# Linear attention stage: another order of the same steps, and constant products at other places

## The reference

```python
mix_in = tanh((x + xx * maa_x) @ maa_w1)            # xx = previous row - row
xrg, xwa, xk, xv = x + xx * (maa + mix)             # four mixed inputs
r, k, v, g, kk, a, ... = products of these          # "features"
def step(S, inp):                                   # per head, 64x64 state
    sa = einsum('bhij,bhj->bhi', S, at)
    S = S * exp(w) + sa * bt + vt * kt
    return S, einsum('bhij,bhj->bhi', S, rt)
y = layernorm_per_head(scan(step)) * ln_w + ln_b + (sum(r*k*faaaa)) * v
out = (y * g) @ w_output.T
```

## Time and profile before

| | |
|---|---|
| median of 3 runs | 3612.98 us (3612.59 to 3615.72) |
| time of the profiled execution | 3623.5 us |
| its span, first to last instruction | 3621.8 us |
| PE, DVE, ACT, POOL busy | 83%, 70%, 50%, 29% of the span |
| mean granted PE clock | 0.912 |
| `stage_c`, first product to last step | 1762 to 3184 us of the span |
| I0 of unit 0 to I9 of unit 15 | 1828 to 3126 us |

### The profile page before, as it was taken

The page is one execution under the profiler, slowest core; times in us unless marked ns, Lnnn a source line. Parts: engine busy times, 40 slices in busy tenths (PEclk is TensorE's granted clock), DMA queues, the critical chain, the costliest instruction groups (busy, mean ns, idle before and its releaser), DMA issues.

```text
span 3621.8 us, 117698 instructions
## 1 busy us (share of the span) xinstructions
PE 3013.2 (83%) x51890; PEld 1965.8 (54%) x51890; DVE 2536.8 (70%) x5294; ACT 1820.5 (50%) x3063; POOL 1047.3 (29%) x1164
## 2 busy tenths in 40 slices
PE   6889999998648898988578888888888887779995
PEld 4555555555325555554245555555555555458774
DVE  3666666665549888888467777787777776457774
ACT  3334444444438878887244444454454552246661
POOL 0332122122531111222232332233333332045552
PEclk8899899899769999999789998899999997789997
DMA  2227999200043444330200000000000000056666
GB/s 75 79 97 304 395 394 319 30 1 1 33 138 128 137 143 140 129 126 21 70 3 4 12 11 9 10 10 13 10 10 10 10 12 14 9 190 228 224 214 180
DMA packets 161678, 356.92 MB, mean 99 GB/s; under 512 B 13821, under 2 KB 98559, under 8 KB 154896
## 3 DMA queue, kind: packets, MB, share of 16 engines
q1 hardware_dynamic: 147088, 323.95, 26.3%
q0 software_dynamic: 14080, 25.45, 2.1%
HBM read 136.33 MB, written 216.67 MB: 97 GB/s over the span
## 4 chain that ended last, share of the span: by engine, by line
PE 54%; DVE 21%; ACT 12%; issue 9%; DMA 2%; SPq 1%; another core or an unknown queue 1%; POOL 1%; DVEq 0%; POOLq 0%; ACTq 0%
PE ps L1551 7%; PE ps L135 4%; PE ps L137 4%; PE ps L136 4%; DVE t L485 3%; PE ps L1616 3%; PE ps L342 2%; PE ps L896 2%; ACT t L1035 2%; ACT t L1033 2%; PE ps L346 2%; PE ps L903 2%; PE ps L298 1%; PE ps L304 1%; DVE t L522 1%
## 5 line engine op out<-in xcount | busy, mean ns | idle before, releaser
L1551 PE MATMUL ps<-t 128*128 128x512 f32 x608 | 345.5, 682 | 49.7 <-DVE t L2056 13.0
L241 POOL TENSOR_SCALAR_AFFINE_SELECT t<-t 128x512 f32<-128x512 f32 x256 | 168.6, 659 | 663.4 <-ACT t L425 663.4
L485 DVE TENSOR_REDUCE t<-ps 128x2 f32<-128x512 f32 (+1 forms) x512 | 260.7, 551 | 116.5 <-PE ps L304 116.3
L135 PE MATMUL ps<-t 128*128 128x512 f32 (+1 forms) x660 | 280.6, 425 | 60.1 <-DVE t L511 34.9
L425 ACT ACTIVATE t<-ps 128x768 f32<-128x768 f32 x256 | 206.8, 808 | 213.1 <-PE ps L330 213.1
L137 PE MATMUL ps<-t 128*128 128x512 f32 (+1 forms) x660 | 258.5, 392 | 0.0
L136 PE MATMUL ps<-t 128*128 128x512 f32 (+1 forms) x660 | 258.2, 391 | 0.0
L1361 POOL DMA_INDIRECT deltas<-t x92 | 94.4, 1026 | 507.1 <-DVE t L1307 484.9
L2794 POOL DMA_INDIRECT answers<-t x156 | 153.9, 987 | 160.3 <-DVE t L2765 122.4
L1551 PEld LDWEIGHTS ps<-t 128*128 128x128 f32 x608 | 111.5, 207 | 142.9 <-issue 75.5
L135 PEld LDWEIGHTS ps<-t 128*128 128x128 f32 x660 | 128.4, 194 | 110.5 <-DVE t L511 42.9
(11 more groups left out here) (443 smaller groups left out, 8359.8 us busy)
## 6 DMA issues: line engine op xcount, KB each, us to landing
paired<-t SPq DMA_DIRECT2D x14, 8384.0 KB, 59.9
t<-experts SPq DMA_DIRECT2D x39, 1536.0 KB
sorted<-t SPq DMA_DIRECT2D x22, 1950.0 KB, 8.8
t<-in_wP SPq DMA_DIRECT2D x92, 320.5 KB, 3.5
experts<-t SPq DMA_DIRECT2D x8, 1536.0 KB, 6.0
t<-sorted SPq DMA_DIRECT2D x39, 260.0 KB
t<-answers SPq DMA_DIRECT2D x16, 512.0 KB, 6.7
t<-in_wE SPq DMA_DIRECT2D x8, 768.0 KB, 7.6
```

The lines of the kernel that those rows point to most:

```text
L135: pe.e.matmul(out, a[0], b[0], start=start, stop=False, skip_group_check=True)
L241: pool.e.affine_select(own, own, [[0, 2], [0, 2], [1, 128]], ALU.is_ge, 0.0, base=0, channel_multiplier=-1).then_inc(*kept(b, j))
L485: m = dve.e.tensor_reduce(nmf[:, z, blk * 16 + 4 * g + i0:blk * 16 + 4 * g + i0 + 2], ps[:, k:k + 2, a0:a1], AX.X, ALU.max, negate=True)
L1551: pe.e.matmul(ps[out, k, :], lhs, rhs, start=True, stop=True).then_inc(*e_pe(u, name))
```

## The change

The two tables get other numbers, nothing else. Every step, its instructions and its waits stay; the places, and so the order on each engine, are others. The first place of a unit is -228 and the last 316, so it lives for 544 places and not for 589. The constant products go from 7 with 1,536 columns for a unit to 11 with 2,944: I2 from (0, 0, 128, 0) to (384, 384, 256, 128), I9 from (384, 0, 0, 0) to (128, 0, 256, 0), the state scan from (384, 128, 128, 256, 128, 0) to (256, 0, 384, 384, 256, 0), and 128 columns at the selection's ranks.

```diff
-AT = {"E": (-243, -236, -219, -216, -208, -198, -188, -183, -179, -170, -162, -151, -147, -138, -136, -133, -132,
-           -131, -122, -121, -120, -116, -114, -113, -111, -108, -102, -99, -91),
-      "L": ((-97, -94, -93, -89, -84, -75, -72, -69, -66, -65, -63, -58, -56, -55, -48, -47, -46),
-            (-40, -37, -35, -34, -30, -29, -28, -25, -23, -22, -16, -15, -14, -8, -2, -1, 14)),
-      "I": ((-26, -20, -19, -11, -6, 1, 9, 13, 20, 29),
-            (3, 10, 12, 21, 28, 35, 42, 52, 58, 71),
-            (38, 50, 51, 59, 65, 76, 81, 87, 95, 105),
-            (79, 85, 86, 96, 102, 111, 117, 120, 126, 134)),
-      "S": (142, 153, 157, 161, 164, 172, 175, 181, 184, 191, 194, 200, 202, 205, 212, 215, 222, 227, 232, 237, 238,
-           245, 259, 266, 269, 271, 273, 284, 287, 307, 308, 324, 331, 337, 346)}
-HOLD = {"tp": (0, 0, 128, 0), "bd": (384, 0, 0, 0), "s": (384, 128, 128, 256, 128, 0),
-        "fc": 0, "rl": 0, "rk": 0}
+AT = {"E": (-228, -220, -210, -206, -200, -197, -193, -186, -174, -165, -160, -154, -146, -137, -130, -128, -123,
+           -122, -121, -119, -114, -108, -101, -100, -97, -94, -92, -91, -87),
+      "L": ((-85, -84, -81, -80, -74, -70, -57, -56, -51, -50, -49, -45, -43, -41, -40, -35, -33),
+            (-32, -31, -30, -28, -25, -24, -23, -20, -18, -11, -7, -4, -3, -2, 0, 6, 28)),
+      "I": ((-21, -14, -13, -10, -1, 5, 13, 27, 34, 42),
+            (12, 25, 26, 31, 35, 45, 52, 62, 69, 77),
+            (50, 60, 61, 67, 72, 78, 86, 94, 101, 109),
+            (84, 91, 92, 99, 104, 112, 119, 126, 132, 140)),
+      "S": (149, 152, 158, 167, 177, 181, 187, 193, 197, 201, 203, 209, 211, 212, 213, 218, 223, 234, 238, 259, 261,
+           267, 271, 279, 280, 283, 285, 294, 297, 298, 299, 308, 309, 312, 316)}
+HOLD = {"tp": (384, 384, 256, 128), "bd": (128, 0, 256, 0), "s": (256, 0, 384, 384, 256, 0),
+        "fc": 0, "rl": 0, "rk": 128}
```

## The result

On the chip of the first measurement the kernel after takes 3682.53 us (median of 4, 3675.58 to 3704.9) and the kernel before 3614.35 us (median of 4): a ratio of 1.0196, 95% interval 1.0157 to 1.0234. It is 2% slower. The forecast was 3585 us, with a range that ended at 3628.

A forecast was written before the change was run, and what follows sets the result against it. PE's order was taken to bound the kernel. Terms a unit: +2.6 - 1.9 - 1.2 - 1.5 = -2.0 us; over 14 units -28 us off the 3612.98 us median, so 3585 us, range 3558 to 3628.

The forecast's parts named there:

- The failed step: Linear attention stage: steps, transfers and waits only move, POOL's scatters with them; no term in the sum.
- nearly all these gaps: PE's "issue" gaps, 96 us in the steady stretch, nearly all at the same place in a row of 256 instructions.
- What bounds the kernel: Linear attention stage: PE's order sets the 82.4 us a unit; DVE has 20 us to spare.
- Constant products: 1,408 more columns a unit on PE: +2.6 us if paid in full, bounds 0 and 5.2.
- rival A: Constant products paid in full, little given back: +2.0 us a unit, 3641 us; above 3620 us, chance 0.23.
- Fetch gaps: Moved constant products fill PE's waits for instruction fetches: -1.9 us a unit, bounds 0 and -2.6.
- The scaling by 7.9 / 13.5: Cuts the fetch-gap gain from -2.2 to -1.3 us a unit, since waits and slow clock fill part.
- Clock: Fewer thin stretches of PE work, 4 of 9.9 us leave the lower clock: -1.2 us a unit, bounds 0 and -4.9.
- Waits: PE's waits for other engines: 3.9 us a unit go, half kept, 0.5 charged: -1.5, bounds +1.0 and -3.9.
- the list of tight pairs: Places where PE has less work between a result and its use, among them DVE's copies and the tanh (0.3 us).
- Ends: First and last units' serial chains at the stage's ends: 0 change, within 5 us either way.
- Rival C: Clock nearly always full, waits nearly gone: -6.0 us a unit, 3529 us; below 3560 us, chance 0.12.

The follow-up runs named there:

- the bunched runs: Kernel before with its last seven S places side by side at 287 to 293: 3675.59 us (1.0117) on chip 3, 3666.48 us (1.0134) on chip 12.

## Why the prediction failed, point by point

**The failed step** is "No step, instruction of a step or transfer is added or removed; POOL's scatters and all waits are moved with their steps", which gave the moved scatters no term in the sum. POOL stands there with 316 busy us of 1000 and no more. What a scatter does to PE wasn't asked, though seven of the eight had moved into one row beside small products. On the first chip that is +9.4 us a unit at I0 of tile 1, more than all terms of the forecast together; behind it the clock has fallen to 0.50. Undone alone, on chip 3, it gives back 1.0025 in place of 1.0196 on the first chip (no run of the unchanged kernel after stands in that group, so the step between the two, 1.7%, is across chips). Done alone it costs 1.17 and 1.34%. None of the rivals had this mechanism. The trace of before did show it, faintly: 26 of its 98 longer "issue" gaps, 12 us in 1000, are not at the place of the fetches, and all 26 lie beside a scatter. The prediction's "nearly all these gaps" (87% of their time) passed over them. The number of matmuls alone gives no warning: 12.1 in a scatter's 1.26 us (18.1 on chip 4), mostly beside products over all 128 rows, which take their time anyway.

The other steps can be read where the scatters cost nothing, on chip 4 (per unit; idle and busy of the windows times the period over 1000):

| | forecast | chip 4 | first chip |
|---|---|---|---|
| "issue" waits of PE | -1.9 | 6.9 to 3.2: **-3.7** | 7.9 to 9.8: **+1.9** |
| waits for other engines | -1.5 | 3.8 to 2.7: **-1.2** | 4.3 to 0.9: **-3.4** |
| constant products and clock, PE busy | +2.6 - 1.2 | 69.7 to 70.1: **+0.4** | 69.9 to 76.8: **+6.9** |
| sum = change of the period | -2.0 | **-4.6** | **+5.3** |

- *What bounds the kernel*: right. Of the 76.2 us of a unit after on chip 4, PE is busy for 70.1 and DVE, the next fullest, for 61.9.
- *Constant products*, "+2.6 us a unit if paid in full": with the table after and its scatters at 339 to 385 they cost nothing on chip 6 (0.9876 with the new, 0.9877 with the old). Their columns fall into time in which PE would have waited for instructions (its issue waits are 53.9 us with the new and 68.0 with the old in 1000) or run in the lower clock. On the table before, on chip 3, they cost 0.9 us a unit, and beside the slow I0 perhaps more (1.0196 against 1.0130, across chips): there rival A may be true in part.
- *Fetch gaps*: the direction was right and the size too small, even against the unscaled -2.2. The scaling by 7.9 / 13.5 for waits that fill part of the short runs made it smaller still. The gaps at every 256th instruction fell on the first chip as well, by the table above from 82 x 0.0824 = 6.8 to 33 x 0.0877 = 2.9 us a unit; the +1.9 there is this and 12 x 0.0824 = 1.0 to 75 x 0.0877 = 6.6 us beside scatters.
- *Clock*: 0.95 to 0.96 on chip 4. Time in the lower clock falls from (1 - 0.95) x 2 x 80.8 = 8.1 to 6.1 us a unit; work of 2.0 us there takes 1.0 above. -1.0 against -1.2: right, within the two digits of the view (the clock records of the two traces give 8.8 to 5.7 us, so -1.6). On the first chip it goes the other way, 9.9 to 19.3 us, as the stall at I0 comes every unit and full products and state products behind it run at half speed.
- *Waits*: those named all went. On the first chip more than forecast went, as one would expect of a PE that loses 9 us at one place and is late everywhere else. On chip 4 a wait came up that wasn't in the list of tight pairs: I3's second product for DVE's state step (L1645 for L2233, 16.3 us, 11 times). The waits that were in it, I3 for DVE's copies and E5 for the tanh, cost nothing.
- *Ends*, "0, within 5 us either way": from the stage's first product to I0 of unit 0 it is now 74.9 instead of 66.1 us (72.9 instead of 65.9 on chip 4), and from I9 of unit 15 to the next stage 62.2 instead of 60.1 (60.4 instead of 55.9). So 11 us are lost at the ends on either chip, outside the bounds. The chain of the first unit's features is not all that sets its start: its steps also stand behind others in the order.
- *The sum on chip 4*: from I0 of unit 0 to I9 of unit 15 it is 1210.8 in place of 1267.4 us, -56.6; ends +11.5; the stages ahead differ by 2 us. Together -47, as measured (3583 to 3536 us). The forecast of -28 us, 0.992, lies above the ratio found there, 0.9865, and its range from 3558 us (0.985) holds it. That it fits there is in part luck: the gain in fetch gaps was twice the forecast's, and the ends took 11 us of it back.
- *Rival C*, "Half of that is 3557": half of -84 us is 3571; 3557 is the middle between the forecast and C. No term or chance hangs on it.

So what failed on the first chip is not the account of fetches, clock and waits but a cost that the change brought with POOL's steps. Times from chip 4 alone would not have shown it. What stays open: why chips 3 and 12 and that of the first measurement (its number isn't known) have it, and 4, 6, 10 and 13 haven't (each was met once, so a condition of the hour isn't excluded); what part of POOL's indirect transfer does it; and what the order with scatters beside full products gives on a chip with the slow issue, since it ran on chips 6, 4, 13 and 10 alone. On chip 4 it can't be told from the kernel after (0.9860 against 0.9865). That it would spare PE on a chip with the slow issue is argued from the bunched runs, where full products lost nothing, and was not measured. Its scatters don't stand beside full products alone, either: on chips 13 and 10 PE starts 44 matmuls on average in a scatter's 1.26 us, small ones for the most part.

## What to carry to other kernels

When an order is changed, look at what each engine's *neighbours* do at the new place, and at transfers issued by POOL first. A row of indirect transfers beside 96 small matmuls cost up to 9.4 us; set apart, they cost less (1.0025 on one chip against 1.0196 on another); beside long matmuls they should cost least, which was not measured where it counts. Count the "issue" gaps by the place of the instruction behind them: here those at every 256th, few and up to 2.7 us long, went with the fetches; what was left over, pieces of up to 1.2 us with a handful of matmuls between them, lay beside POOL's transfers, and 12 us of it in the trace of before became 75 in the trace of after. Measure an order on more than one chip before you call it better: the same two kernels stood at 1.020 on one and 0.987 on another.

## What the runs showed of the hardware that was not expected

- On some chips (3, 12, and that of the first measurement) PE gets 3 to 5 matmuls and as many weight loads in 0.72 to 1.43 us while POOL issues an indirect transfer each 1.26 us; on chips 4, 6, 10 and 13 neighbouring small ones start 11 to 12 ns apart all the same. Even the kernel before, with its scatters well placed, differs: 3614 to 3634 us where the issue is slow (82.4 us a unit on the first chip), 3569 to 3583 us where it isn't (80.8 on chip 4).
- The first 51 matmuls of I0 still pass at full rate, in 0.87 us from just before the first scatter's start; only then does the crawl begin. In the bunched kernel, too, 41 to 44 small ones pass before it. That PE has about that many instructions in store would fit both and was not tried.
- A plain transfer from SP of the same rows costs PE nothing that the times show on either: 3519 to 3529 us in five measurements on five chips, with 139 GB/s beside small products.
- A POOL indirect transfer shows 0.96 us in the trace (1.03 for the first of a row), but its packets come after that: from 1.6 to 2.0 us after the first one's start. The Trainium skill ("Perfetto Trace Analysis", DMA Instruction — SWDGE (GPSIMD)) says that the end shown is that of descriptor generation, not of the movement of data; the trace agrees.
